# An RWKV mix and SwiGLU layer on one core: round 1's second half in another order, chunk 2's V projection from one mixed half, three low parts on VectorE

## What is computed

```python
xk = x * time_mix_k + xx * (1.0 - time_mix_k)      # xv and xr in the same way
k, v = xk @ Wk.T, xv @ Wv.T
sr = sigmoid(xr @ Wr.T)
rwkv = sr * wkv(-exp(time_decay), time_first, k, v) # a recurrence over the 4096 rows, stable in the log domain
x = layernorm(x + rwkv @ Wo.T)
g, u = x @ (w_gate / 127).T, x @ (w_up / 127).T     # 768 hidden channels, integer weights
out = layernorm(x + (silu(g) * u) @ (w_down / 127).T)
```

## Time and profile before

| | us |
|---|---|
| median of 3 runs | 288.36 (288.19 to 288.69) |
| the profiled execution's own time | 287.45 |
| its span (first to last instruction) | 285.6 |
| PE busy | 272.8 |
| DVE busy | 263.6 |
| ACT busy | 213.3 |
| POOL busy | 188.0 |

### The profile page before, as it was taken

How to read it: one execution, slowest core, us unless ns; L and a number is a source line. 1 busy time by engine, 2 the same in 40 slices (tenths; PEclk the granted TensorE clock), 3 DMA queues, 4 the chain that set the end, 5 groups by cost and what they waited for, 6 DMA issues and landing times.

```text
span 285.6 us, 4294 instructions
## 1 busy us (share of the span) xinstructions
PE 272.8 (96%) x1258; PEld 198.8 (70%) x1258; DVE 263.6 (92%) x454; ACT 213.3 (75%) x383; POOL 188.0 (66%) x153
## 2 busy tenths in 40 slices
PE   8999999978999999999999999999999999999891
PEld 6654667445875679558874789468965789778791
DVE  5999998999999999999899999999999999888874
ACT  3698874868856986698957986798868982699482
POOL 3738698699978775986688675887476580325051
PEclk9999999999999999999999999999999999999998
DMA  7922200203004001220204020210201020102003
GB/s 236 379 84 75 77 0 0 75 2 110 0 2 147 2 29 47 73 74 0 73 5 147 0 73 0 75 36 0 75 25 50 0 76 0 37 2 75 0 3 115
DMA packets 13573, 16.26 MB, mean 57 GB/s; under 512 B 752, under 2 KB 11248, under 8 KB 13552
## 3 DMA queue, kind: packets, MB, share of 16 engines
q1 hardware_dynamic: 12720, 15.35, 16.5%
q10 hardware_dynamic: 832, 0.66, 0.7%
HBM read 11.81 MB, written 4.19 MB: 56 GB/s over the span
## 4 chain that ended last, share of the span: by engine, by line
PE 63%; ACT 5%; DVE 4%; issue 4%; POOL 2%; DVEq 0%; POOLq 0%; ACTq 0%
PE bank_a L1232 12%; PE bank_b L1232 12%; PE bank_a L1255 11%; PE bank_b L1188 7%; PE bank_c L1139 6%; PE bank_d L1139 6%; PE bank_a L1139 6%; PE bank_b L1209 2%; POOL hlo L411 1%; DVE stats L817 1%; ACT L624 1%; ACT x L533 1%; POOL wts L383 1%; DVE rwkv L810 1%; ACT hhi L604 1%
## 5 line engine op out<-in xcount | busy, mean ns | idle before, releaser
L411 POOL TENSOR_TENSOR hlo<-hid,hhi 128x512 fp32r<-128x512 f32 (+1 forms) x39 | 56.8, 1463 | 33.8 <-ACT hhi L604 33.6
L383 POOL TENSOR_SCALAR wts<-gap,par 128x512 f32<-128x512 f32 (+1 forms) x18 | 35.2, 1956 | 22.3 <-DVE gap L737 21.4
L1255 PE MATMUL bank_a<-wd_r,hhi 128*128 128x256 f32 x180 | 44.7, 290 | 0.1
L1255 PE MATMUL bank_a<-wd_r,hlo 128*128 128x256 f32 x180 | 42.6, 279 | 0.0
L518 ACT ACTIVATE mix<-dx,par 128x512 f32<-128x512 f32 x44 | 28.7, 713 | 17.5 <-POOL dx L363 17.5
L369 POOL TENSOR_TENSOR mix<-mix,xt 128x512 f32<-128x512 f32 (+1 forms) x36 | 39.4, 1131 | 3.0 <-DVE shift L866 2.7
L1255 PEld LDWEIGHTS bank_a<-wd_r,hhi 128*128 128x128 f32 x180 | 33.8, 188 | 2.8 <-issue 2.1
L1232 PE MATMUL bank_a<-x1hi,wg_r 128*128 128x512 f32 (+1 forms) x96 | 32.4, 417 | 3.1 <-ACT x1hi L589 2.3
L510 ACT ACTIVATE wts<-wts 128x512 f32<-128x512 f32 (+1 forms) x54 | 28.1, 580 | 8.9 <-DVE wts L746 8.1
L1255 PEld LDWEIGHTS bank_a<-wd_r,hlo 128*128 128x128 f32 x180 | 33.8, 188 | 0.7 <-issue 0.7
L604 ACT ACTIVATE hhi<-hid 128x512 fp32r<-128x512 f32 (+1 forms) x53 | 30.7, 581 | 4.3 <-DVE hid L886 4.2
(11 more groups left out here) (130 smaller groups left out, 588.4 us busy)
## 6 DMA issues: line engine op xcount, KB each, us to landing
xrow<-x SPq DMA_DIRECT2D x7, 512.0 KB, 3.7
xt<-xT SPq DMA_DIRECT2D x6, 513.0 KB, 3.6
out<-y_buf SPq DMA_DIRECT2D x6, 512.0 KB, 2.9
wg_i<-wg SPq DMA_DIRECT2D x1, 768.0 KB, 7.9
wu_i<-wu SPq DMA_DIRECT2D x1, 768.0 KB, 9.3
wd_i<-wd SPq DMA_DIRECT2D x1, 768.0 KB, 11.1
out<-y_buf SPq DMA_DIRECT2D x3, 256.0 KB, 2.3
y_buf<-xT SPq DMA_DIRECT2D x1, 513.0 KB, 10.1
```

The lines of the kernel that those rows point to most:

```text
L383: nc.gpsimd.tensor_scalar(wts[:, OUT, h, 0:n], gap[:, h, 0:n], par[:, FIRST, h:h + 1], CAP, ALU.add, ALU.min).then_inc(out_arg_ready, 1)
L411: nc.gpsimd.tensor_tensor(hlo[:, m, 0:n], hid[:, m % NH, 0:n], hhi[:, m, 0:n].bitcast(f32), ALU.subtract).then_inc(hlo_ready, 1)
L1255: mm = nc.tensor.matmul(ffn[:, q, :], hp.bitcast(f32) if full else hp, w[:, m, :], start=(m == 0 and q % 2 == 0 and part is hhi), stop=(m ...
```

## The change

Two edits, both of round 1 (the loop's steady rounds are as before).

The V half of chunk 2: POOL mixes its input half h = 0 ahead of round 1 (`mixing(2, 0, V, 0)`), and PE multiplies this mixed half directly (`v2_mixed`, two instructions); only for h = 1 are there still two passes (`v2_last_step`, `v2_change`, two instructions each). Six matrix instructions stand where eight stood. The low parts 3, 4 and 5 of chunk 0 move from POOL to DVE (`low_part_first`), one ahead of `gate_num` and two ahead of `divide`, with a semaphore of their own. In the second half of round 1, DVE, ACT and POOL do their steps in another order: DVE makes the gaps and exponent arguments of half 0 earlier and those of half 1 behind `x1_low`; ACT takes one exponential, then `x1_high`, then the others; POOL mixes only K of chunk 3 ahead of `out_arg`, and V and R behind it, after a wait for all of chunk 2's exponent arguments.

```diff
@@ POOL, round_
-                    for m in range(NM if j == 1 else NP):
+                    for m in range(NH if j == 1 else NP):
                         low_part(j - 1, m)
...
                     if j == 1:
                         mixing(2, 0, R, 0)
-                        mixing(2, 0, R, 1, 2 * CH + 1)
+                        mixing(2, 0, R, 1, CH + 2)
                     else:
                         diffs(j + 2)
                     if j == 1:
+                        pool.wait_ge(mv2_ready, NT)
+                        mixing(3, s, K, 0)
                         pool.wait_ge(shift1_ready, 2)
-                    mix_chunk(j + 2, s, [K, V] if j == 1 else range(3))
+                        mixing(3, s, K, 1)
+                    else:
+                        mix_chunk(j + 2, s)
...
                 if j == 1:
-                    mix_chunk(3, s, [R])
+                    pool.wait_ge(args_ready, 3 * (2 * CH))
+                    mix_chunk(3, s, [V, R])
@@ POOL, ahead of round 1
             for h in range(CH):
                 pool.wait_ge(r1_mixed, h + 1)
                 diff(2, h)
+            mixing(2, 0, V, 0)
@@ ACT, first_norm
                 norm1(j)
+                if isinstance(j, int) and j == 1:
+                    weights(2, 0, [IN_NEW])
+                    x1_high(1, 0)
+                    x1_high(1, 1)
+                    weights(2, 0, [IN_OLD, OUT])
+                    rstd(0, mv2, lnv2, rstd2, mv2_ready, lnv2_ready, rstd2_ready)
+                    weights(2, 1)
+                    return
@@ DVE
+            def low_part_first(m):
+                dve.wait_ge(hhi_ready, m + 1)
+                n = steps(0)
+                nc.vector.tensor_tensor(hlo[:, m, 0:n], hid[:, m % NH, 0:n], hhi[:, m, 0:n].bitcast(f32),
+                                        ALU.subtract).then_inc(hlo0_ready, 1)
...
                 numerator(j)
+                if j == 1:
+                    low_part_first(NH)
...
                     gate_num(j)
+                    if j == 1:
+                        low_part_first(NH + 1)
+                        low_part_first(NH + 2)
...
                 running_max(j + 1, 0)
                 shift_rows1(j)
+                if j == 1:
+                    gaps(2, 0)
+                    running_max(2, 1)
+                    exp_args(2, 0)
+                    gaps(2, 1)
+                    x1_low(1, 0)
+                    x1_low(1, 1)
+                    exp_args(2, 1)
+                    shift_rows2(0)
+                    return
@@ PE
+            def v2_mixed():
+                pe.wait_ge(mixed, 1)
+                pe.wait_ge(num_parts, 2)
+                for d in range(CH):
+                    nc.tensor.matmul(bank_d[:, d, :], wvT[:, 0, d * P:(d + 1) * P], mix[:, 0, V, 0, :],
+                                     start=True, stop=False)
...
                     gate_up(0, range(2, 4), full)
-                    project_last_step(2, V, [0])
+                    v2_mixed()
                     gate_up(0, range(4, NM), full)
-                    project_last_step(2, V, [1])
+                    v2_last_step()
...
                     down(0, range(2), full)
-                    project_change(2, 0, V, [0])
-                    down(0, range(2, 4), full)
-                    project_change(2, 0, V, [1])
-                    down(0, range(4, NM), full)
+                    v2_change()
+                    down(0, range(2, NM), full)
```

More of the change, by code:

```diff
@@ L223, in rwkv_swiglu_kernel @@
         hlo_ready = sem("hlo_ready")
+        hlo0_ready = sem("hlo0_ready")
         hlo_last_ready = sem("hlo_last_ready")
@@ L271, in lows_ahead @@
         def lows_ahead(c):
-            return c * NP if first(c) else c * NP + (NM - NP)
+            return c * NP if first(c) else c * NP + (NH - NP)
         def place(c, i):
@@ L882, in product @@
                     dve.wait_ge(hlo_ready, lows_ahead(c) + (m - NH + 1))
-                elif c == 1 or (m < NH - (NM - NP) and not first(c)):
+                elif c == 1:
+                    dve.wait_ge(hlo0_ready, m + 1)
+                elif m < NH - (NM - NP) and not first(c):
                     dve.wait_ge(hlo_ready, lows_ahead(c - 1) + (m + NM - NH + 1))
@@ L1155, in project_first, with project_last_step @@
                             mm.then_inc(ready, 1)
-            def project_last_step(c, i, halves=range(CH)):
+            def project_last_step(i, halves=range(CH)):
                 w, bank = ((wkT, bank_a), (wvT, bank_d), (wrT, bank_c))[i]
-                pe.wait_ge(xt_in if c == 1 else xt2_in, 16)
+                pe.wait_ge(xt_in, 16)
                 if i == K:
@@ L1163, in project_last_step, with project_change @@
                 else:
-                    pe.wait_ge(num_parts, c)
+                    pe.wait_ge(num_parts, 1)
                 for d in halves:
                     for h in range(CH):
-                        mm = nc.tensor.matmul(bank[:, d, :], w[:, h, d * P:(d + 1) * P], xt_of(c)[:, h, 0:N],
+                        mm = nc.tensor.matmul(bank[:, d, :], w[:, h, d * P:(d + 1) * P], xt[:, h, 0:N],
                                               start=(h == 0), stop=False)
-                if c == 1 and i == V and halves[-1] == CH - 1:
+                if i == V and halves[-1] == CH - 1:
                     mm.then_inc(last_steps_done, 1)
-            def project_change(c, s, i, halves=range(CH)):
+            def project_change(i, halves=range(CH)):
                 w, bank, ready = ((wkT, bank_a, k_ready), (wvT, bank_d, v_ready), (wrT, bank_c, r_ready))[i]
@@ L1176, in project_change, with v2_last_step, v2_change @@
                     for h in range(CH):
-                        pe.wait_ge(dx_scaled, (c - 1) * (3 * CH) + place(c, i) * CH + h + 1)
-                        mm = nc.tensor.matmul(bank[:, d, :], w[:, h, d * P:(d + 1) * P], mix[:, s, i, h, :],
+                        pe.wait_ge(dx_scaled, i * CH + h + 1)
+                        mm = nc.tensor.matmul(bank[:, d, :], w[:, h, d * P:(d + 1) * P], mix[:, 1, i, h, :],
                                               start=False, stop=(h == CH - 1))
                     mm.then_inc(ready, 1)
+            def v2_mixed():
[4 more added lines that the diff above has]
+                                     start=True, stop=False)
+            def v2_last_step():
+                pe.wait_ge(xt2_in, 16)
+                for d in range(CH):
+                    nc.tensor.matmul(bank_d[:, d, :], wvT[:, 1, d * P:(d + 1) * P], xt_of(2)[:, 1, 0:N],
+                                     start=False, stop=False)
+            def v2_change():
+                pe.wait_ge(dx_scaled, 3 * CH + place(2, V) * CH + 2)
+                for d in range(CH):
+                    nc.tensor.matmul(bank_d[:, d, :], wvT[:, 1, d * P:(d + 1) * P], mix[:, 0, V, 1, :],
+                                     start=False, stop=True).then_inc(v_ready, 1)
             def attention_out(c):
@@ L1245, in down @@
                     pe.wait_ge(hhi_ready, c * NM + (m + 1))
-                    if first(c) or m < NP:
+                    if first(c) and m >= NH:
+                        pe.wait_ge(hlo0_ready, m - NH + 1)
+                    elif first(c) or m < NP:
                         pe.wait_ge(hlo_ready, lows_ahead(c) + (m + 1))
@@ L1313, in round_ @@
                 if first(j):
-                    project_last_step(1, K)
-                    project_change(1, 1, K)
-                    project_last_step(1, V, [0])
+                    project_last_step(K)
+                    project_change(K)
+                    project_last_step(V, [0])
                     pe.wait_ge(wo_in, 16)
```

6 lines of the change are left out of this document (3 added, 3 removed).

## The result

| | us |
|---|---|
| median of 4 runs, changed kernel | 286.50 (286.16 to 286.72) |
| median of 4 runs of before beside them | 288.27 (288.04 to 288.69) |
| ratio | 0.9937, 95% interval 0.9924 to 0.9949 |
| the profiled execution's own time | 286.4 |
| its span | 284.5 |

The forecast was 286.8, with a range of 285.6 to 288.1. Measured are 1.8 us less than before (1.5 to 2.2 by the interval). The two profiled executions are 1.05 us apart (287.45 and 286.4).

A forecast was written before the change was run, and what follows sets the result against it. PE bounds the kernel from 81 us on, DVE and POOL together pace round 2. Of 2.8 us gained, 1.2 go to two extra mixings, leaving 1.6: 285.9 for the profiled execution, plus 0.91 gives 286.8, range 285.6 to 288.1.

The forecast's parts named there:

- early mixing costs DVE's scan: POOL's extra mixing ahead of round 1: DVE's scan already under way, POOL waits, cost nothing; bounds 0 and 0.6 of loss.
- shift of x1's norm: Middle of round 1: DVE's shift comes at 52.9, after 54.30, with ACT's scaling as the late link.
- fifth hidden product: Round 2 on DVE: comes at 72.2, against 73.77 before, after scans and mixings alternate.
- scans of round 2: Sign to look for in round 2: DVE's scans last 1.8 us and more.
- PE's pair: V of chunk 2 on PE: one pair of matrix instructions goes, 1.72 with the switch of 0.40; attention_out(1) at 45.82.
- Low parts on DVE: Round 1: three low parts cost DVE +1.0, silent POOL gives time back; DVE breaks even, rwkv at 45.6.
- The order: DVE's order after the shift, round 1: gate_up(1) at 58.0, first scan of round 2 at 59.2, 2.8 us on both.
- What is late next: Round 2: POOL's four mixings alternate with DVE's scans; two extra mixings take 1.2 of 2.8 us, 1.6 are left.
- DVE alone as the pace: Rival for round 2: POOL does its extra mixings during DVE's PSUM products, time 285.7; chance 0.18.
- The slower case: Rival: late shift plus blocked arguments start round 2's mixings at 62.1, losing from 60.8 on; time 289.7; chance 0.08.
- The early collision: Rival ahead of round 1: POOL's first mixing gets in before DVE's scan, 0.6 lost, time 287.4; chance 0.12.
- The blocked arguments: Rival: exponent arguments issued inside an out_arg stand until its end, mixings start 1.6 later, time 288.4; chance 0.12.

The follow-up runs named there:

- the version with both V mixings early: The change with both of chunk 3's V mixings put ahead of out_arg in round 1: 285.93, ratio 0.9913; once more 285.57, ratio 0.9904.
- the second's: The change itself, unaltered, timed once more against the kernel before: 286.77, ratio 0.9958 (0.9941 to 0.9976).

## Why the prediction was right

Right by its own steps, with these numbers against the record:

| step | forecast | measured |
|---|---|---|
| early mixing costs DVE's scan | nothing, scan 1.4 | 1.41; mixing 2.20 |
| attention_out(1) | 45.82 | 45.79 |
| rwkv ready | 45.6 | 45.4 |
| shift of x1's norm | 52.9 | 52.74 to 53.04 |
| gate_up(1) | 58.0 | 57.45 |
| first scan of round 2 | 59.2 | 58.94 |
| fifth hidden product | 72.2 | 72.32 |
| attention_out(2) earlier by | 1.6 | 1.45 |
| profiled execution | 285.9 | 286.4 |
| time | 286.8 | 286.5, again 286.77 |
| scans of round 2 | 1.8 and more | 1.27, 1.67, 2.12, 1.46 |

- *PE's pair.* 1.72 forecast; 47.54 - 45.79 = 1.75 measured, and 1.72 from round 1's first scan. The run without the V part shows that all of the gain hangs on it.
- *Low parts on DVE.* The break-even at the divide held: 1.00 us of new work against 1.08 back from a silent POOL. The run without them shows PE held at 46.85.
- *The order.* 2.8 us forecast for gate_up and the scan; 3.4 and 3.0 measured. Part of this is PE's pair again: by the run without the new order, and from round 1's first scan on, the order itself brings 1.9 to gate_up(1) and 1.5 to the scan. The forecast has 1.2 of the 2.8 given back and 1.6 left. That these 1.6 are the pair's alone, and that the order's part is given back whole, the prediction did not say; only the runs show it. gate_up was mis-sized by 0.5: ACT had its x1hi ready at 56.5, and I had placed it at 56.7 and let PE wait for both parts of x1lo.
- *What is late next.* The taking of turns was the right mechanism, but not the turns as I had them. I let the first mixing go ahead of the first scan; the scan started 0.1 us sooner (58.94, the mixing 59.04), kept its 1.27, and the mixing waited. So the four mixings took 7.46 us where I had 6.5, and DVE was further ahead than forecast: its fourth scan ended at 67.5 where I had 69.05, and the long wait came at the fourth hidden product and not at the fifth. The two errors cancel, which is luck. The mixings ended 0.9 us late, den_sum ended at 69.7 where I had 70.05, and the fifth hidden product came 0.1 late.
- *Rivals.* DVE alone as the pace (285.7) fell: the 1.80 us of waiting. The slower case had its threshold at mixings from 60.8 on; they started at 59.04. The early collision fell: scan 1.41. The blocked arguments fell: the pair took 0.92 beside an out_arg of 54.30 and lasted 1.22 beside the next, so nothing stood for 2 us. By those rows the rule of the Trainium skill ("SBUF — State Buffer", "Who interferes with whom") that a `tensor_scalar` in a two-port mode and a GpSimd instruction exclude each other did not act between these two. Arguments beside mixings did stand: 2.20 for the pair in the version with both V mixings early. The same section of the Trainium skill says that a VectorE instruction with two SBUF inputs contends with a GpSimd instruction that reads SBUF. The scans beside mixings agree (2.32 at 63.79); a scan beside an out_arg, which reads SBUF too, does not: the one of 61.97 to 63.21 cost its 1.24 us inside this out_arg, a row of the chain of the kernel before (start, us, what):

```profile
61.53 2.01 POOL wts L383
```

- *Lucky in part.* The time's gain of 1.8 us in the first measurement is more than the trace's 1.45, the second's 1.2 less. Executions of the kernel before differ by 1.2 us and more, so the last tenths are not evidence for the steps; the positions in the trace are. The forecast put the profiled execution at 285.9 and added the 0.91 by which the one of before lay under its median; the one of the change took 286.4 and lay 0.1 under. The first term was 0.5 too low, the second 0.8 too high, and the sum came out 0.3 off.

## What to carry to other kernels

Count the instructions of VectorE and GpSimd that read two SBUF operands as one queue, and sum them over the stretch that paces the program: here 1.1 us for each 128x512 mixing on GpSimd, and 1.4 for each when VectorE made them (16.67 to 19.39 us for the two, 0.3 of it a wait for ScalarE). A reorder that starts such a stretch earlier gave nothing here, as it also put more of them into it. What did pay was to move them to a stretch where VectorE could wait for them: its first scan came 1.3 us later, and the program was faster.

When work is deferred on a shared queue, follow the last consumer, not only the one that waits now: the mixings moved behind the third low part freed VectorE and stalled TensorE 3.1 us at the fourth.

## What the runs showed that I had not expected

In some executions a wait of TensorE was followed by a fall of its clock. In the kernel with the R mixings on DVE and the old order, PE stood idle for 1.33 us in 72 to 74 us and for 0.39 in the next two; then its granted clock fell to 0.50 and 0.73 in the next two stretches, and attention_out(2) started 2.9 us after the divide had, where it is 1.6 in the change: some 1.3 us lost. A wait is not enough for it. The version with both V mixings early has the same 1.53 us wait at the same place in both of its profiles: one then has 0.50 in 66 to 68 us (0.988 over the span), the other keeps 1.00 there. The fall cost 0.3 us up to attention_out(2) (a distance of 32.89 us from attention_out(1), against 32.62); DVE and POOL pace that stretch. And the profile of the version with the R mixings behind the third low part keeps 1.00 through its 3.1 us wait. Which of these waits lets the clock fall stays open.

That last version measured 287.5 in three executions and 288.7 to 289.3 in nine. Of the nine, five have a mean granted clock of 0.986 or 0.987, which none of the three has (0.992 to 0.997); the other four have 0.991 or 0.992. So a fall of the clock goes with a part of the slower ones, but no profile of one was taken, and it does not explain all.
